# Graph layers with attention: half of the attention stage's lane one-hots kept in DRAM from the adjacency stage

## The chip, the cores and the metric

One core of one Trainium2 chip runs the kernel. The metric is the device time of one execution in microseconds (us). TensorE is PE in the rows (PEld is its weight load), VectorE is DVE, ScalarE is ACT, GpSimd is POOL, and SP is the queue from which most transfers (DMAs) are issued.

## What is computed

There are 3125 nodes of 128 features and 103125 edges, sorted by target. Three rounds of a weighted sparse product are summed and normalised; then a 4-head graph attention over the same edges is added and normalised again.

```python
def spmm(x):                                   # three rounds, summed
    return segment_sum(edge_weight[:, None] * x[src], dst, N)
x = layernorm(x + (x + spmm(x) + spmm(spmm(x)) + ...))
h = (x @ W_node.T).reshape(N, H, HD)           # H = 4, HD = 32
att = leaky_relu(a . [h[src], h[dst], e], 0.2) # per edge and head
m = maximum(segment_max(att, dst), 0)
w = exp(att - m[dst]) / (segment_sum(exp(...)) + (E - deg) * exp(-m))
x = layernorm(x + segment_sum(w * h[src], dst))
```

## The kernel before, in words

Nodes are cut into `NB` = 25 blocks of 128 (a node is block number times 128 plus lane). Nothing is gathered by row: each target has up to 64 edges, and for each block a dense matrix from sources to the block's 128 targets is built on PE out of one-hots. A source id is split into lane (low 7 bits) and block (high bits). DVE compares the lane with 0..127, which gives a lane one-hot of 128 by 32 by 128 elements of two bytes (1 MB) for half a block of targets' edges, and the block with 0..25, which gives a small one-hot; the small one is multiplied by the edges' weights, and PE multiplies lane one-hot by weighted block one-hot. A block has two halves, n = 2j and n = 2j + 1.

The stages follow one another, and each engine has its own hand-written order of instructions, tied by semaphores:

- **Adjacency** (some 90 to 460 us of the span). For each half, DVE's `one_hots` writes `L[n % 4]` (lane, line 1153), `Hh` (1155) and six weighted `Hw[n % 2]` (1163), and raises `lh_ready`. PE's `octet` (607) makes four groups of results for a half, in two PSUM banks; ACT copies each (889) into `rows[j % 2]` and raises `oct_sb`. SP stores the block with four DMAs into `adj` (292); ACT must see that store landed before it writes the same `rows` buffer two blocks later. In between PE, ACT and SP also work on the edge attributes: SP loads them in pairs of DMAs of 992 KB (250), one pair every second block up to block 15. SP also stores each block's source ids (`dup`) into `lh_d` (275).
- **Layers** (to about 880 us): PE multiplies by `adj`, read back in pieces. **Scores** (to about 1075 us): attention terms of the sources.
- **Attention** (to the end). SP loads the ids back (`lhd`, 366). For each half, DVE's `weighted` writes `Lq[n % 2]` (lane again, from the same ids, 1339), `Hq` (1341) and eight `Hx[n % 2]` (1346), and raises `hx_ready`. Around the two halves DVE also does `logits_of`, `finish` and `weights_of` of other blocks. PE's `weights_set` (746) makes 16 sets for a block, 0 to 7 from the even half and 8 to 15 from the odd one, with pieces of the product of the block before (757) between them; after set 8 it turns the next block's weights (732). ACT copies each set (1009), computes exponentials after set 3 and, after set 9, writes the next block's duplicated weights `wdup` (998), on which the next even `weighted` waits.

The odd half's `Lq` holds the same zeros and ones as the odd half's `L` of the adjacency stage; `L` is bf16 and `Lq` fp16. The two waits on which the order around the change rests are in `weighted`:

```python
                if hf == 0:
                    dve.wait_ge(s[f"lhd{j % 3}"], 16 * (j // 3 + 1))
                    dve.wait_ge(s["wdup_sb"], j + 1)
                if n >= 2:
                    dve.wait_ge(s["set_ps"], 8 * (n - 1))
```

Of the kernel before, what the change touches and what calls it, by code (L numbers as in the profile page):

```python
# [36 lines left out]
HP = U // 2  # L37
# [29 lines left out]
def build(nc, x, src, dst, edge_attr, edge_weight, w_node, w_edge, att, out):  # L67
# [5 lines left out]
    rec_d = dram("rec_d", (P * RW + U, REC), BF16)  # L73
    adj = dram("adj", (NB, P, HIP * P), F32)
    lh_d = dram("lh_d", (NB, P, 2 * U * 2), BF16)
    slp = dram("slp", (2, NT, P), BF16)
    z_d = dram("z_d", (E + U, H), F32)
    g_x = [dram(f"g_x{l}", (TBL, D), F32) for l in range(LAYERS + 1)]
# [2 lines left out]
    with ctx:  # L81
# [82 lines left out]
        with ExitStack() as c:  # L164

            Att = [sb(f"Att{i}", [P, H * NB, P], F32, c) for i in range(2)]
            Lq = [sb(f"Lq{i}", [P, HP, P], F16, c) for i in range(2)]
            Hq = sb("Hq", [P, 2, HP, HIP], F16, c)
            Hx = [sb(f"Hx{i}", [P, 2, HP, H, HIP], F16, c) for i in range(2)]
            lhd = sb("lhd", [P, 3, 2, U, 2], BF16, c)  # L170
            zr = sb("zr", [P, 3, U, H], F32, c)
            am = sb("am", [P, 2, H, U], F32, c)
            am2, ex = sb("am2", [P, 2, H, U], F32, c), sb("ex", [P, 2, H, U], F32, c)
            Z16 = sb("Z16", [P, 2, 2, H, P], F16, c)
            wdup = sb("wdup", [P, 2, 2 * H, U, 2], F16, c)
            mx, sm = sb("mx", [P, 2, H], F32, c), sb("sm", [P, 3, H], F32, c)
            fm, fe = sb("fm", [P, 2, 2, H], F32, c), sb("fe", [P, 2, 2, H], F32, c)
            miss = sb("miss", [P, NB], F32, c)
            scale = sb("scale", [P, NB, H], F32, c)
            oT, on = sb("oT", [P, P], F32, c), sb("on", [P, D], F32, c)  # L180
# [3 lines left out]
        names = """lane_set consts clears ld_f ld_d ld_s ld_w ld_wt ld_x ea0 ea1 diag_ready fb_ps fb_sb bad_sb bad_ps flag_ready  # L184
            wp1 wp2 wp3 wr1 wr2 ints rec_out rowi_ready dr0 dr1 dr2 dr3 dr4 dr_used off_ready wt_ps wt_sb
            eaT_ps eaT_sb eaT_used elog_sb
            recs0 recs1 recs2 z_dve z_act clean j_ps dup_sb dup0 dup1 dup2 lh_ready oct_ps oct_sb adj0 adj1
            ld_st ld_sc lohi_sb lohi_ps slt_sb slp_out pc0 pc1 pc2 pc3 pc4 pc5 pc_used yT_sb yt_ps xb_sb y3_sb less_ready squares
            var_ready std_ready x1_ready x1T_ps x1T_sb h_ps h_sb part_ready
            bc0 bc1 bc2 bc3 bh0 bh1 bh2 bh3 lt_ready p4_ps p4_sb  z_ready z_out z_pad pad_out  # L190
# [30 lines left out]
        def _(sp):  # L221
# [55 lines left out]
            def adjacency():  # L277
                store_dup(0)
                store_dup(1)
                for j in range(NB):  # L280
                    if j + 2 < NB:
                        store_dup(j + 2)
                    g = (j + 9) // 2
                    if j % 2 == 1 and EPRE // NC + 2 <= g < NG:
                        sp.wait_ge(s["eaT_ps"], (g - 1) * NC)
                        load_attr(g)
                    sp.wait_ge(s["oct_sb"], 8 * (j + 1))
                    for c in range(2):
# [25 lines left out]
            def layers():  # L314

                sp.wait_ge(s["elog_sb"], NG)
                sp.wait_ge(s["adj0"], 64 * (NB - NB // 2))
                sp.wait_ge(s["adj1"], 64 * (NB // 2))
                for k in range(3):
                    sp.wait_ge(s[f"dup{k}"], 16 * len(range(k, NB, 3)))  # L320
                for n in range(RING):
                    load_piece(n)
                sp.wait_ge(s["ld_sc"], 1)
                edge_tiles(sp, src_t[:, :], src, s["ld_st"])
                for n in range(RING, RING + 5):
                    load_piece(n)
                sp.wait_ge(s["slt_sb"], 14)
                for k in range(2):
                    for q in range(7):
                        r = min(P, NT - q * P)  # L330
                        sp.dma_start(slp[k, q * P:q * P + r, :], slt[0:r, k, q, :]).then_inc(s["slp_out"], 16)
                for n in range(RING + 5, LAYERS * NCH * NPC - 12):
                    load_piece(n)
                sp.wait_ge(s["slp_out"], 16 * 14)
                for h in range(3):
                    load_half(h)
                for n in range(LAYERS * NCH * NPC - 12, LAYERS * NCH * NPC):
                    load_piece(n)
# [19 lines left out]
                    store_half(h)  # L358

            def attention():  # L360
                for j in range(NB):
                    if j >= 3:
                        sp.wait_ge(s["hx_ready"], 2 * (j - 2))
                    else:
                        sp.wait_ge(s["z_out"], 16 * (NH + 1))
                    sp.dma_start(lhd[:, j % 3, :, :, :].rearrange("p q u k -> p (q u k)"), lh_d[j, :, :]).then_inc(s[f"lhd{j % 3}"], 16)
                for k in range(3):
                    b0, b1 = CUT[k], CUT[k + 1]
                    sp.wait_ge(s["y_sb"], b1)
# [175 lines left out]
        def _(pe):  # L545
# [189 lines left out]
            def weights_set(j, q):  # L735
                n, i = 2 * j + q // 8, 16 * j + q
                if q % 8 == 0:
                    pe.wait_ge(s["hx_ready"], n + 1)
                if i >= 3:
                    pe.wait_ge(s["set_sb"], i - 2)  # L740
                for v in range(4):
                    pp = q % 8 * 4 + v
                    for k in range(2):
                        for d in range(2):
                            rows = slice(d * U, (d + 1) * U)
                            m = pe.matmul(bank[i % 3 * 2 + d][:, v * H * NB:(v + 1) * H * NB].rearrange("p (h i) -> p h i", h=H),  # L746
                                          Lq[n % 2][rows, pp, :], Hx[n % 2][rows, k, pp, :, 0:NB], start=(k == 0), stop=(k == 1))
                m.then_inc(s["set_ps"], 1)

            def product(j, lo, hi):  # L750
# [327 lines left out]
        def _(dve):  # L1078
# [67 lines left out]
            def one_hots(n):  # L1146
# [3 lines left out]
                    dve.wait_ge(s["dup_sb"], j + 1)  # L1150
                if n >= LB:
                    dve.wait_ge(s["oct_ps"], 4 * (n - LB + 1))
                dve.tensor_tensor(L[n % LB][:, :, :].rearrange("p u (n k) -> p u n k", k=2), pair_lo, spread(dup[:, j % 3, 0, us, :], P // 2),  # L1153
                                  ALU.is_equal)
                dve.tensor_tensor(Hh[:, n % 2, :, :].rearrange("p u (n k) -> p u n k", k=2), pair_hi,  # L1155
# [153 lines left out]
            def weights_of(j):  # L1309
# [14 lines left out]
                dve.drain()  # L1324
                dve.reciprocal(sm[:, 1, :], sm[:, 0, :])
                dve.drain()
                dve.scalar_tensor_tensor(out=scale[:, j, :], in0=sm[:, 1, :], scalar=1.0 / UP, in1=fe[:, v, 0, :], op0=ALU.mult, op1=ALU.mult)
                dve.drain()
                dve.sem_inc(s["scale_sb"], 1)

            def weighted(n):
# [4 lines left out]
                    dve.wait_ge(s["wdup_sb"], j + 1)  # L1336
                if n >= 2:
                    dve.wait_ge(s["set_ps"], 8 * (n - 1))
                dve.tensor_tensor(Lq[n % 2][:, :, :].rearrange("p u (n k) -> p u n k", k=2), pair_lo, spread(lhd[:, j % 3, 0, us, :], P // 2),  # L1339
                                  ALU.is_equal)  # L1340
                dve.tensor_tensor(Hq[:, n % 2, :, :].rearrange("p u (n k) -> p u n k", k=2), pair_hi,
                                  spread(lhd[:, j % 3, 1, us, :], HIP // 2), ALU.is_equal)
                dve.drain()
# [216 lines left out]
```

## Time and profile before

| what | value |
|---|---|
| runs of the kernel | 1679.84, 1680.29, 1684.0 us; median 1680.29 |
| profiled execution | 1682.1 us, of which the span is 1680.3 us |
| busy over the span | PE 1396.0 us (83%), DVE 1059.3 (63%), ACT 680.2 (40%) |
| mean granted TensorE clock | 0.908 |
| moved by DMA | 250.32 MB |

The span runs from the first to the last instruction of the profiled execution. Busy shares are averages over stages that have different limits, so the stages are read one by one.

### The profile page before, as it was taken

The numbers are of one execution on the slowest core, as the hardware profiler recorded it, in microseconds if no ns is written. First come the engines' busy times: TensorE is split into PE (matmuls) and PEld (weight loads), VectorE is DVE, ScalarE is ACT, GpSimd is POOL, SyncE is SP. The second block draws the span as 40 slices with busy tenths as digits, with TensorE's granted clock in tenths as the row PEclk, the third lists the DMA queues.
The fourth block names the chain that finished last, engine by engine and source line by source line (L and its number), as shares of the span: only waits on it lengthen the run. The fifth ranks groups of instructions, "written<-read, shape, count | busy, mean of one in ns | idle before, by whom it ended". The sixth has DMA issues, their size and how long they took to land.

```text
span 1680.3 us, 50213 instructions
## 1 busy us (share of the span) xinstructions
PE 1396.0 (83%) x22245; PEld 1008.0 (60%) x22245; DVE 1059.3 (63%) x2069; ACT 680.2 (40%) x1575; POOL 140.0 (8%) x102
## 2 busy tenths in 40 slices
PE   4969899986399999999997998567888886888885
PEld 4968789876344454454446888545555554555554
DVE  5499999999500010000116888788888887888873
ACT  3246565654200000001111000166766777677775
POOL 2611101110000000000000000111111011110000
PEclk9999898998799999999997999768888887788887
DMA  5628677755498879969972776200000000000000
GB/s 198 219 94 243 184 212 204 221 145 132 128 348 317 302 282 339 305 213 370 301 257 78 206 217 205 60 11 12 12 11 10 12 12 11 12 9 13 25 3 23
DMA packets 214644, 250.32 MB, mean 149 GB/s; under 512 B 43578, under 2 KB 146487, under 8 KB 214294
## 3 DMA queue, kind: packets, MB, share of 16 engines
q1 hardware_dynamic: 210422, 236.52, 43.6%
q0 software_dynamic: 4000, 10.54, 2.1%
q8 instruction: 177, 2.90, 0.7%
q14 instruction: 45, 0.37, 0.1%
HBM read 197.88 MB, written 49.14 MB: 147 GB/s over the span
## 4 chain that ended last, share of the span: by engine, by line
PE 47%; DVE 31%; DMA 6%; issue 5%; DVEq 4%; ACT 4%; SPq 1%; ACTq 1%; POOL 0%; POOLq 0%
PE bank L680 24%; PE bank L746 9%; PE bank L757 8%; DVE Hw L1163 8%; DVE L L1153 6%; DVE Hx L1346 5%; DVE Lq L1339 4%; DMA lob<-slp 2%; DVE sel L1278 2%; PE bank L717 2%; DMA drow<-in_dst,rowi 2%; DMA hib<-slp 2%; ACT Att L1009 1%; DVEq L1157 1%; DVE Hh L1155 1%
## 5 line engine op out<-in xcount | busy, mean ns | idle before, releaser
L1009 ACT COPY Att<-bank 128x400 f32<-128x400 f32 x800 | 334.9, 540 | 168.2 <-PE bank L746 167.5
L746 PE MATMUL bank<-Hx,Lq 64*128 64x100 f16 x6400 | 241.3, 223 | 88.9 <-DVE Hx L1346 83.3
L746 PEld LDWEIGHTS bank<-Hx,Lq 64*128 64x128 f16 x6400 | 176.6, 102 | 176.3 <-DVE Hx L1346 90.4
L757 PE MATMUL bank<-Att,xa 128*32 128x128 f32 x5000 | 243.0, 307 | 37.8 <-ACT oT L1016 37.8
L607 PE MATMUL bank<-L,Hw 128*52 128x128 bf16 x4800 | 178.1, 233 | 56.2 <-DVE Hw L1163 53.8
L1346 DVE TENSOR_TENSOR Hx<-Hq,wdup 128x832 f16<-128x832 f16 x400 | 205.3, 588 | 4.1 <-issue 0.4
L607 PEld LDWEIGHTS bank<-L,Hw 128*52 128x52 bf16 x4800 | 154.1, 113 | 65.4 <-DVE Hw L1163 58.7
L1163 DVE TENSOR_TENSOR Hw<-Hh,dup 64x832 bf16<-64x832 bf16 x300 | 176.0, 587 | 8.1 <-PE bank L607 1.1
L889 ACT COPY rows<-bank 116x512 f32<-116x512 f32 x200 | 117.2, 586 | 151.2 <-PE bank L607 142.4
L757 PEld LDWEIGHTS bank<-Att,xa 128*32 128x32 f32 x5000 | 123.8, 117 | 77.5 <-ACT Att L1009 41.6
L717 PE MATMUL bank<-Tp,lob 128*128 128x100 bf16 x2418 | 152.5, 210 | 15.6 <-DVE sel L1278 13.6
L717 PEld LDWEIGHTS bank<-Tp,lob 128*128 128x128 bf16 x2418 | 148.1, 99 | 19.1 <-DVE sel L1278 11.7
L484 POOL DMA_INDIRECT zr<-z_d,off x25 | 63.8, 2552 | 1100.0 <-DMA z_d<-elog 704.8
L680 PE MATMUL bank<-pieces,xs 128*128 128x512 f32 (+1 forms) x350 | 138.3, 555 | 17.6 <-DMA pieces<-adj 17.6
L1339 DVE TENSOR_TENSOR Lq<-iota_lo,lhd 128x4096 f16<-128x4096 bf16 x50 | 114.6, 2292 | 55.7 <-PE bank L746 51.4
L719 PE MATMUL bank<-far,hib 128*128 128x100 bf16 x806 | 148.2, 209 | 0.0
L680 PE MATMUL bank<-pieces,xb 128*128 128x512 f32 (+1 forms) x350 | 137.6, 548 | 0.4 <-ACT xb L969 0.4
L680 PE MATMUL bank<-pieces,xa 128*128 128x512 f32 (+1 forms) x350 | 135.6, 547 | 0.4 <-ACT xa L969 0.4
L578 PEld LDWEIGHTS bank<-wedge,eaT 128*128 128x128 f32 (+1 forms) x832 | 127.3, 230 | 1.1 <-issue 0.2
L578 PE MATMUL bank<-wedge,eaT 128*128 128x8 f32 (+1 forms) x832 | 123.6, 273 | 0.0
L924 ACT COPY yT<-bank 128x512 f32<-128x512 f32 (+1 forms) x21 | 11.3, 540 | 269.6 <-PE bank L680 269.6
L680 PEld LDWEIGHTS bank<-pieces,xs 128*128 128x128 f32 x350 | 63.2, 193 | 88.3 <-issue 88.1
(174 smaller groups left out, 1362.8 us busy)
## 6 DMA issues: line engine op xcount, KB each, us to landing
pieces<-adj SPq DMA_DIRECT2D x90, 1280.0 KB, 8.9
adj<-rows SPq DMA_DIRECT2D x100, 416.0 KB
lob<-slp SPq DMA_DIRECT2D x26, 992.0 KB, 6.2
ea<-in_edge_attr SPq DMA_DIRECT2D x25, 992.0 KB, 8.1
hib<-slp SPq DMA_DIRECT2D x78, 64.0 KB, 4.8
pieces<-adj SPq DMA_DIRECT2D x15, 320.0 KB, 3.1
lh_d<-dup SPq DMA_DIRECT2D x25, 64.0 KB, 3.9
lhd<-lh_d SPq DMA_DIRECT2D x25, 64.0 KB, 1.8
```

Source lines behind the costliest of these rows:

```text
L578: m = pe.matmul(bank[7][:, (k * SH + u) * H:(k * SH + u + w) * H], eaT[0:w * DE, q % ER, n * P:(n + 1) * P], wedge[0:w * DE, 0:w * H], sta ...
L607: mm = pe.matmul(bank[m % 2][c * U:c * U + 2 * HIP, v * P:(v + 1) * P], Hw[n % 2][:, k, pp, :, :].rearrange("p d i -> p (d i)"), L[n % LB] ...
L680: m = pe.matmul(bank[n % 2][:, 0:w], cur[:, b, :], rhs, start=(b == 0), stop=(b == NB - 1))
L717: pe.matmul(o, lob[:, h % 4, t * P:(t + 1) * P], Tp[:, k, :, :].rearrange("p h i -> p (h i)"), start=(k == 0), stop=False)
L719: m = pe.matmul(o, hib[:, h % 4, t // 4, :], far[:, t % 4, :, :].rearrange("p h i -> p (h i)"), start=False, stop=True)
L746: m = pe.matmul(bank[i % 3 * 2 + d][:, v * H * NB:(v + 1) * H * NB].rearrange("p (h i) -> p h i", h=H), Lq[n % 2][rows, pp, :], Hx[n % 2][ ...
L757: m = pe.matmul(bank[7][h * HD:(h + 1) * HD, 0:P], xa[:, i, h * HD:(h + 1) * HD], Att[j % 2][:, h * NB + i, :], start=(i == 0), stop=(i == ...
L889: act.copy(rows[j % 2][0:U + 2 * HIP, hf * 4 + o, :, :].rearrange("p v n -> p (v n)"), bank[m % 2][0:U + 2 * HIP, :])\
L1009: m = act.copy(o[:, d, :, :], bank[i % 3 * 2 + d][:, 0:4 * H * NB].rearrange("p (q i) -> p i q", q=4))
L1163: m = dve.tensor_tensor(Hw[n % 2][rows, k, :, d, :].rearrange("p u (n k) -> p u n k", k=2), Hh[rows, n % 2, :, :].rearrange("p u (n k) -> ...
L1339: dve.tensor_tensor(Lq[n % 2][:, :, :].rearrange("p u (n k) -> p u n k", k=2), pair_lo, spread(lhd[:, j % 3, 0, us, :], P // 2), ALU.is_equal)
L1346: m = dve.tensor_tensor(Hx[n % 2][:, k, :, h, :].rearrange("p u (n k) -> p u n k", k=2), Hq[:, n % 2, :, :].rearrange("p u (n k) -> p u n ...
```

## The change

In the adjacency stage each odd half's lane one-hot, `L[1]` or `L[3]`, is stored to a new DRAM tensor `lo_d` by SP, before the block's `adj` stores. DVE may write that `L` buffer again, two blocks later, only when its store has landed. In the attention stage DVE writes only the even `Lq`; the odd one is loaded by SP from `lo_d`, once PE has used the odd half before it, and PE's set 8 waits for it. The bits of bf16 1.0 read as fp16 are 1.875, so `Lq` is now bf16, PE reads it as fp16, and the final scale is divided by 1.875. SP issues the loads of ids two blocks ahead of the `Lq` loads. Nothing else of the computation changes.

```diff
+    lo_d = dram("lo_d", (NB, P, HP * P), BF16)
...
-            Lq = [sb(f"Lq{i}", [P, HP, P], F16, c) for i in range(2)]
+            Lq = [sb(f"Lq{i}", [P, HP, P], BF16, c) for i in range(2)]
...
                         load_attr(g)
+                    sp.wait_ge(s["lh_ready"], 2 * j + 2)
+                    sp.dma_start(lo_d[j, :, :], L[(2 * j + 1) % LB][:, :, :].rearrange("p u n -> p (u n)"))\
+                        .then_inc(s[f"lo_out{(2 * j + 1) % LB}"], 16)
                     sp.wait_ge(s["oct_sb"], 8 * (j + 1))
...
             def attention():
-                for j in range(NB):
+                def ids_in(j):
...
+                ids_in(0)
+                ids_in(1)
+                for j in range(NB):
+                    if j + 2 < NB:
+                        ids_in(j + 2)
+                    if j:
+                        sp.wait_ge(s["set_ps"], SETS * j)
+                    sp.dma_start(Lq[1][:, :, :].rearrange("p u n -> p (u n)"), lo_d[j, :, :]).then_inc(s["lo_in"], 16)
...
                     pe.wait_ge(s["hx_ready"], n + 1)
+                    if n % 2:
+                        pe.wait_ge(s["lo_in"], 16 * (j + 1))
...
                     dve.wait_ge(s["oct_ps"], 4 * (n - LB + 1))
+                    if n % 2:
+                        dve.wait_ge(s[f"lo_out{n % LB}"], 16 * (n // LB))
...
-                dve.tensor_tensor(Lq[n % 2][:, :, :].rearrange("p u (n k) -> p u n k", k=2), pair_lo, spread(lhd[:, j % 3, 0, us, :], P // 2),
-                                  ALU.is_equal)
+                if hf == 0:
+                    dve.tensor_tensor(Lq[0][:, :, :].rearrange("p u (n k) -> p u n k", k=2), pair_lo, spread(lhd[:, j % 3, 0, us, :], P // 2),
+                                      ALU.is_equal)
```

SP's queue in the adjacency stage, from the ids' store of one block to that of the next, where a pair of attribute loads (`ea`) falls. Before:

```order
L275 DMA lh_d<-dup 128x256 [waits dup_sb]
L250 DMA ea<-in_edge_attr_64 128x1984 [waits eaT_ps]
L250 DMA ea<-in_edge_attr_64 128x1984
L292 DMA adj<-rows1 26x32x128 [waits oct_sb]
L292 DMA adj<-rows1 26x32x128 x3
```

and now:

```order
L277 DMA lh_d<-dup 128x256 [waits dup_sb]
L252 DMA ea<-in_edge_attr_64 128x1984 [waits eaT_ps]
L252 DMA ea<-in_edge_attr_64 128x1984
L290 DMA lo_d<-L3 128x4096 [waits lh_ready]
L297 DMA adj<-rows1 26x32x128 [waits oct_sb]
L297 DMA adj<-rows1 26x32x128 x3
```

The 1 MB store stands in front of the block's four `adj` stores, with a wait of its own.

DVE in the attention stage, from one even half's `weighted` through `logits_of` to the odd half's, now:

```order
L1360 TENSOR_TENSOR Lq0<-iota_lo,lhd 128x4096 [waits set_ps,wdup_sb,lhd1]
L1362 TENSOR_TENSOR Hq<-iota_hi,lhd 128x832
L1367 TENSOR_TENSOR Hx0<-Hq,wdup 128x32x26 x8
L1310 TENSOR_TENSOR am<-zr,sdst 128x256 [waits e_sb,zr0]
...
L1325 TENSOR_SCALAR fm<-mx 128x4
L1362 TENSOR_TENSOR Hq<-iota_hi,lhd 128x832 [waits set_ps]
L1367 TENSOR_TENSOR Hx1<-Hq,wdup 128x32x26 x8
```

Before, a row `Lq1<-iota_lo,lhd` stood ahead of the second `Hq`, and the wait on `set_ps` was on it.

SP's queue at the start of the attention stage, now:

```order
L373 DMA lhd<-lh_d 128x256 [waits z_out] x3
L382 DMA Lq1<-lo_d 128x4096
L373 DMA lhd<-lh_d 128x256 [waits hx_ready]
L382 DMA Lq1<-lo_d 128x4096 [waits set_ps]
L373 DMA lhd<-lh_d 128x256 [waits hx_ready]
L382 DMA Lq1<-lo_d 128x4096 [waits set_ps]
```

Before, only the loads of `lhd` stood there, with the same waits.

## Rows read from the trace of the kernel before

**Rows 1.** Busy time of each engine by stretch: two adjacency blocks, then attention.
```profile
core 0: us, PE busy (x) PEld busy (x) DVE busy (x) ACT busy (x) POOL busy (x), PEclk, DMA share, GB/s
126.00:154.00 28.00, 26.40 (x538) 24.74 (x538) 27.21 (x39) 17.97 (x37) 3.48 (x2) 1.00 0.82 230
...
1060.00:1660.00 600.00, 459.71 (x11674) 319.23 (x11671) 489.89 (x1010) 402.38 (x977) 63.80 (x25) 0.83 0.05 13
```

**Rows 2.** Waits from 1060 to 1660 us: total us, times, longest.
```profile
PE bank L746 <- DVE Hx L1346: 83.3, 27, 11.0
...
DVE Lq L1339 <- PE bank L746: 51.4, 23, 7.4
```

**Rows 3.** Timelines of DVE, PE and ACT in an attention block: start, us, idle before.
```profile
1310.87 2.29 DVE L1339 TENSOR_TENSOR Lq<-iota_lo,lhd 128x4096 f16<-128x4096 bf16 x1 [2.31 <-PE bank L746]
...
1317.90 0.85 PE L746 MATMUL bank<-Hx,Lq 64*128 64x100 f16 x16 [2.76 <-DVE Hx L1346]
...
1320.87 2.29 DVE L1339 TENSOR_TENSOR Lq<-iota_lo,lhd 128x4096 f16<-128x4096 bf16 x1
...
1323.74 4.11 DVE L1346 TENSOR_TENSOR Hx<-Hq,wdup 128x832 f16<-128x832 f16 x8
...
1329.00 0.54 PE L746 MATMUL bank<-Hx,Lq 64*128 64x100 f16 x16
...
1331.74 1.04 ACT L998 CAST wdup<-bank 128x1024 f16<-128x1024 f32 x1
```

**Rows 4.** Timeline at set 8 of attention's first block, and of block 14.
```profile
1108.36 0.85 PE L746 MATMUL bank<-Hx,Lq 64*128 64x100 f16 x16 [2.79 <-DVE Hx L1346]
...
1111.35 1.03 ACT L998 CAST wdup<-bank 128x1024 f16<-128x1024 f32 x1
...
1428.61 0.54 PE L746 MATMUL bank<-Hx,Lq 64*128 64x100 f16 x16 [2.40 <-DVE Hx L1346]
...
1433.05 2.29 DVE L1339 TENSOR_TENSOR Lq<-iota_lo,lhd 128x4096 f16<-128x4096 bf16 x1 [1.35 <-ACT wdup L998]
```

**Rows 5.** Groups by line, 1060 to 1660 us: the lane one-hots.
```profile
L1339 DVE TENSOR_TENSOR Lq<-iota_lo,lhd 128x4096 f16<-128x4096 bf16 x50 | 114.6, 2292 | 55.7 <-PE bank L746 51.4 <-ACT wdup L998 1.4 <-issue 0.2
```

**Rows 6.** Timeline of SP's queue in two adjacency blocks: start, us spent issuing.
```profile
238.98 1.34 SPq L250 DMA_DIRECT2D ea<-in_edge_attr  x2
240.58 13.42 SPq L292 DMA_DIRECT2D adj<-rows  x4
...
258.31 5.54 SPq L292 DMA_DIRECT2D adj<-rows  x4
```

**Rows 7.** Stretches of the adjacency stage, columns as in rows 1.
```profile
240.60:247.60 7.00, 6.22 (x125) 5.75 (x125) 6.81 (x10) 4.21 (x9) 2.31 (x1) 1.00 0.93 301
...
277.50:294.00 16.50, 15.00 (x247) 13.99 (x246) 16.11 (x21) 8.18 (x17) 2.45 (x1) 0.79 0.71 191
...
347.00:361.00 14.00, 11.94 (x247) 11.07 (x243) 13.61 (x20) 8.49 (x18) 2.73 (x1) 1.00 0.51 134
```

**Rows 8.** DMA busy tenths in 40 slices of 268:296 (with GB/s), then of 449:460.
```profile
DMA  4959999998888994776676688677868744765120
GB/s 126 187 197 374 397 363 363 329 329 305 265 271 252 275 307 140 206 189 154 185 200 179 143 244 223 154 166 206 191 181 253 244 138 140 195 174 148 40 88 6
...
DMA  0566666666667767777887665326777666651000
```

**Rows 9.** Chain that ended last, from 85 to 480 us: start, us, what.
```profile
347.97 2.29 DVE L L1153
...
362.12 2.29 DVE L L1153
...
452.73 6.87 DMA adj<-rows
```

**Rows 10.** Waits from 95 to 460 us: total us, times, longest.
```profile
ACT rows L889 <- DMA adj<-rows: 4.5, 4, 1.5
...
DVE Hw L1163 <- PE bank L607: 1.1, 2, 0.7
```

**Rows 11.** DMA issues: count, KB each, median us to landing.
```profile
ea<-in_edge_attr SPq DMA_DIRECT2D x25, 992.0 KB, 8.1
```

More of the change, by code:

```diff
@@ L57 @@
 UP = float(2 ** 14)
+ONE = 1.875
 FAR = -float(2 ** 127)
@@ L186, in build @@
             eaT_ps eaT_sb eaT_used elog_sb
-            recs0 recs1 recs2 z_dve z_act clean j_ps dup_sb dup0 dup1 dup2 lh_ready oct_ps oct_sb adj0 adj1
+            recs0 recs1 recs2 z_dve z_act clean j_ps dup_sb dup0 dup1 dup2 lh_ready lo_out1 lo_out3 lo_in oct_ps oct_sb adj0 adj1
             ld_st ld_sc lohi_sb lohi_ps slt_sb slp_out pc0 pc1 pc2 pc3 pc4 pc5 pc_used yT_sb yt_ps xb_sb y3_sb less_ready squares
@@ L320, in layers @@
                     sp.wait_ge(s[f"dup{k}"], 16 * len(range(k, NB, 3)))
+                sp.wait_ge(s["lo_out1"], 16 * (NB - NB // 2))
+                sp.wait_ge(s["lo_out3"], 16 * (NB // 2))
                 for n in range(RING):
@@ L746, in weights_set @@
                             m = pe.matmul(bank[i % 3 * 2 + d][:, v * H * NB:(v + 1) * H * NB].rearrange("p (h i) -> p h i", h=H),
-                                          Lq[n % 2][rows, pp, :], Hx[n % 2][rows, k, pp, :, 0:NB], start=(k == 0), stop=(k == 1))
+                                          Lq[n % 2][rows, pp, :].bitcast(F16), Hx[n % 2][rows, k, pp, :, 0:NB], start=(k == 0), stop=(k == 1))
                 m.then_inc(s["set_ps"], 1)
@@ L1326, in weights_of @@
                 dve.drain()
-                dve.scalar_tensor_tensor(out=scale[:, j, :], in0=sm[:, 1, :], scalar=1.0 / UP, in1=fe[:, v, 0, :], op0=ALU.mult, op1=ALU.mult)
+                dve.scalar_tensor_tensor(out=scale[:, j, :], in0=sm[:, 1, :], scalar=1.0 / (ONE * UP), in1=fe[:, v, 0, :], op0=ALU.mult, op1=ALU.mult)
                 dve.drain()
```

## The prediction, made before the changed kernel ran

> **What bounds the kernel now.** I read the busy time by stage first. In the adjacency stage DVE is busy 27.21 of 28 us, and the DMA engines 0.82 of the time; in attention DVE is the busiest too, but with 489.89 of 600 us it has gaps [rows 1]. So the two stages that the change touches have different limits, and I follow each by its waits.
>
> In attention the waits say who holds whom: PE waits for DVE's `Hx` 83.3 us, in only 27 waits for 50 halves, and DVE's `Lq` waits 51.4 us, in 23 [rows 2]. One block shows why [rows 3]. The even `Lq` starts at 1310.87; `Hq` and `Hx` follow, and PE's set 0 starts at 1317.90, after 2.76 us without work. The odd `Lq` starts at 1320.87, and the odd `Hx` are done at 1323.74 + 4.11 = 1327.85. PE comes to set 8 only at 1329.00, without having waited. After sets 8 and 9 ACT writes `wdup`, done at 1331.74 + 1.04 = 1332.78, and only then can the next even `Lq` start. (The row at 1310.87 names PE as releaser of its 2.31 us wait, but PE's even sets were long done; in the program that instruction waits for `wdup` as well.) The loop of a block is therefore even `Lq`, `Hx`, sets 0 to 9, `wdup`. The odd `Lq` hangs beside it, with 1.15 us to spare.
>
> In adjacency I read DVE's step from the chain: `L` of two blocks starts at 347.97 and 362.12, so a block takes 14.15 us [rows 9].
>
> **The change, part by part.**
>
> *25 odd `Lq` go from DVE.* One takes 2.292 us [rows 5], so DVE loses 57.3 us of work. In a block like that of rows 3 all of it lies beside the loop: the odd `Hx` are ready 2.3 us sooner, PE arrives at set 8 when it did, and DVE waits for `wdup` longer. I cost these blocks at nothing; what is next late there is still the even half. The odd half is on the path where PE stood at set 8: in the first block, 2.79 us, and in block 14, 2.40 us, behind the first normalisation [rows 4]. There the whole 2.29 us comes out, because `wdup` follows set 9 directly (1111.35 after a set 8 at 1108.36; `Lq` at 1433.05 after a set 8 at 1428.61). **Minus 4.6 us.** The bounds are 0 and minus 5.2 (the two waits whole).
>
> *25 loads of 1 MB into `Lq[1]`.* SP issues one when PE has done the odd half before, some 14 us ahead of the set 8 that needs it (set 15 ends just before the 2.76 us without work that end at 1317.90, and set 8 is at 1329.00 [rows 3]). A load of 992 KB lands in 8.1 us in the median, amid other traffic [rows 11]; attention moves 13 GB/s [rows 1]. I take nothing. The bounds are 0 and, if it took over 14 us, the excess in each block. The loads of ids keep their waits, and what waits behind them in SP's queue is only the output's stores, due at the end. The even `Lq` is of the same width as before: nothing. The scale's constant: nothing.
>
> *25 stores of 1 MB in adjacency.* This is the dear part. DVE issues nothing for them, and its new wait (for a store two blocks old) has 28 us. But they stand in SP's queue before the `adj` stores, and that queue is nearly full. The last block's `adj` stores, with nothing beside them, keep the DMA engines at 6 to 7 tenths for 36 slices of 0.275 us, which is 9.9 us [rows 8]; so 6 to 7 tenths is what these stores look like at full speed. Behind a pair of attribute loads two blocks' stores run back to back at the same 0.71 [rows 7]. Over 268 to 296 us, which is one pair of attribute loads and two blocks' stores, data flows without a break but for about the last 2.5 us [rows 8]: 25.5 us of work in 28.3 us. SP is held back accordingly: it needs 13.42 us to issue one block's four stores behind the attributes [rows 6].
>
> A store of 1.05 MB takes 3.5 us at the 301 GB/s of the attribute loads [rows 7] and 2.6 us at the highest slice, 397 GB/s [rows 8]. I take 2.7, near the slice, since in a full queue the start of one transfer hides behind the one before. Two blocks then ask for 25.5 + 2 x 2.7 = 30.9 us of 28.3: 2.6 us too much, in each of the eight pairs of blocks that load attributes: 21 us. After block 16 a block asks for 9.9 + 2.7 and a little for ids, under 14.15, so there it costs nothing.
>
> Not all of the 21 us reaches DVE. Late `adj` stores hold ACT at the `rows` buffer, ACT holds PE, and PE holds DVE, which may be a half-block ahead: 7 us. ACT itself has some 2 us, since it waited only 4.5 us so far, and DVE's `Hw` waited for PE 1.1 us in the whole stage [rows 10]. So **plus 21 - 9 = 12 us.** The bounds: 0, if the stores slip into the third of the engines' time that rows 8 show free; and 34 us, with 3.5 us a store (8 x 4.2) and no cushion.
>
> The Trainium skill (DMA: Bandwidth & Descriptors, Specifications) gives a ceiling of 435 GB/s, and by it a store would take 2.4 us, an estimate from that page. The excess would be 2.0 us a pair, the cost 16 - 9 = 7 us and the whole change +2.4 us. The trace's 301 GB/s stay well below that ceiling.
>
> The end of the stage: the last `adj` stores land 6.87 us after their last issue [rows 9]; the last 1 MB store is issued before them, while PE works on the last half, and I give it nothing.
>
> *Sum:* 12 - 4.6 = +7.4 us. The profiled execution took 1682.1 us, with a span of 1680.3, so it would take 1689.5; it stood 1.8 us above the median of the runs. From the median, 1680.29 + 7.4 = **1687.7 us**.
>
> **The rivals.**
>
> *The stores cost nothing.* If the idle third of the engines' time during `adj` stores can be used, only the 4.6 us are left: 1675.7 us, so not slower. For it: the mean DMA share of a block without attributes is only 0.51 [rows 7]. Against it: the 0.71 behind the attributes, where the queue was full. It decides as soon as a store takes under some 2 us of the queue's time (21 becomes 9, the cushion).
>
> *No cushion.* PE waits more, and has no time to catch up: its granted clock is 0.79 in one such stretch already, so part of it at the lower of its two levels, 1.2 and 2.4 GHz [rows 7]. That is +34 - 4.6 = 1709.7 us at the most; I put it at 1704.
>
> *The load is late.* If `lo_in` came 2 us after PE reaches set 8, 24 blocks would lose 2 us each: 1724 us. A load would have to take over 14 us where 8.1 is the median in worse traffic.
>
> *DVE's work counts in full.* 57.3 us less, 1623 us. It needs every odd `Hx` to hold PE; the counts of rows 2 (27 waits, 25 blocks) and the 1.15 us to spare in rows 3 contradict it. The Trainium skill (Trace Analysis, Identifying the Most-Contended Engine) would lead here: it says to take the engine with the highest occupancy as the most contended and to optimise it first, and that is DVE in attention. On the waits, this trace does not agree.
>
> **How the numbers follow.** A measurement of this kernel tells 0.3%, 5 us, from no change. The forecast case has a chance of 0.47 and runs from 1682 to 1698; of it 0.38 lies above 1685.3 and 0.09 in the middle. Free stores have 0.36: 0.22 within 5 us of before, 0.14 below it. No cushion has 0.12, a late load 0.03, DVE in full 0.02. That makes faster 0.16, same 0.31, slower 0.53. The range goes from 1675 (free stores) to 1704 (no cushion); it leaves out the last two rivals, the best of the free stores and the upper end of the third.
>
> **What would show it.** In the changed kernel: attention blocks of the same length, DVE's wait before the even `Lq` some 2.3 us longer, and no wait at set 8 in the first block and in block 14. In adjacency: more than 4.5 us of ACT waiting for `adj<-rows`, DVE's `Hw` or `L` waiting for PE, and the stage's end some 12 us later, all of it before block 17. I am wrong if the pieces of `adj` start by 460 us as before (free stores), or if PE waits for a DMA at set 8.

## The result, and the profile after

| what | before | after |
|---|---|---|
| median of 10 runs each | 1679.68 us | 1689.74 us |
| lowest to highest | 1677.49 to 1684.0 | 1686.15 to 1693.98 |
| profiled execution | 1682.1 us (span 1680.3) | 1693.98 us (span 1692.2) |
| busy: PE, DVE, ACT | 1396.0, 1059.3, 680.2 us | 1392.8, 1005.0, 675.8 us |
| moved by DMA | 250.32 MB | 302.77 MB |

The ratio is 1.0059, with a 95% interval of 1.0046 to 1.0072: slower by 9.9 us (7.7 to 12.1). The profiled executions stand above their medians, by 2.4 us before and by 4.2 us after, so the traces show some 2 us more as lost than the medians do.

DVE has 54 us less to do and the kernel is slower. The two stages tell why, one at a time.

**Adjacency.** First the end of the stage, the issue of the first pieces of `adj`, in SP's timelines (start, us spent issuing). Before:

```profile
459.65 11.31 SPq L300 DMA_DIRECT2D pieces<-adj  x6
```

After (with the first and the last block that load attributes, and some of the blocks behind them):

```profile
130.25 12.86 SPq L297 DMA_DIRECT2D adj<-rows  x4
...
345.38 12.47 SPq L297 DMA_DIRECT2D adj<-rows  x4
...
362.34 10.03 SPq L297 DMA_DIRECT2D adj<-rows  x4
...
376.01 6.69 SPq L297 DMA_DIRECT2D adj<-rows  x4
...
388.15 9.40 SPq L297 DMA_DIRECT2D adj<-rows  x4
...
477.69 10.37 SPq L305 DMA_DIRECT2D pieces<-adj  x6
```

The stage ends 18.0 us later. The rows of blocks 1 and 15 lie seven pairs of blocks apart: (345.38 - 130.25) / 7 = 30.73 us a pair. The same two in the kernel before, with blocks 3 and 16:

```profile
129.52 10.30 SPq L292 DMA_DIRECT2D adj<-rows  x4
...
155.25 9.56 SPq L292 DMA_DIRECT2D adj<-rows  x4
...
325.04 8.68 SPq L292 DMA_DIRECT2D adj<-rows  x4
...
339.20 7.82 SPq L292 DMA_DIRECT2D adj<-rows  x4
```

That is 27.93 us a pair: 2.8 us less on the mean. The first of these pairs took only 25.73 us (129.52 to 155.25); the six behind it took (325.04 - 155.25) / 6 = 28.30 us each, which is DVE's pace of 2 x 14.15. In block 16, SP is 362.34 - 339.20 = 23.1 us behind. From block 17 on it catches up, with a step of 12 us from block 17 to 18 (376.01 to 388.15) where DVE's block takes 14.15.

Who waits for the late queue is in the waits of after, from 95 to 475 us (total us, times, longest):

```profile
ACT rows L907 <- DMA adj<-rows: 66.5, 16, 8.3
...
DVE L L1173 <- DMA lo_d<-L: 13.4, 6, 3.2
...
DVE Hw L1183 <- PE bank L623: 4.8, 7, 1.1
...
DVE L L1173 <- PE bank L623: 1.0, 1, 1.0
```

ACT waits 66.5 us for `adj` stores, where it had waited 4.5 [rows 10]. DVE, which had waited 1.1 us in the whole stage, now waits 13.4 + 4.8 + 1.0 = 19.2 us: 18.1 more, which is the 18.0 of the stage's end. Most of it is its own new wait, for the store of `lo_d`. Where it lies is in DVE's timeline; these are `L` of the even halves of blocks 18 and 19:

```profile
364.06 2.29 DVE L1173 TENSOR_TENSOR L<-iota_lo,dup 128x4096 bf16<-128x4096 bf16 x1
...
380.18 2.29 DVE L1173 TENSOR_TENSOR L<-iota_lo,dup 128x4096 bf16<-128x4096 bf16 x1
```

Blocks 18 and 19 stood at 347.97 and 362.12 [rows 9]: 16.1 and 18.1 us late. The whole 18 us are reached only here, three blocks behind the last attribute load. A row of the DMA issues of 268 to 296 us, the stretch of [rows 8] (count, KB each, median us to landing):

```profile
lo_d<-L SPq DMA_DIRECT2D x2, 1024.0 KB, 9.5
```

A store of one-hots takes 9.5 us from issue to landing there.

**Attention.** The waits from 1080 to 1680 us of after:

```profile
DVE Lq L1360 <- PE bank L764: 84.1, 23, 8.6
PE bank L764 <- DVE Hx L1367: 79.1, 26, 10.6
...
DVE Z L1335 <- ACT Z L1009: 15.3, 20, 0.9
```

DVE waits 32.7 us longer ahead of the even `Lq` (51.4 in [rows 2]), and PE only 4.2 us less for `Hx`. DVE's wait for ACT's `Z` (15.3 us in 20 waits) is new: it comes to it sooner than ACT has it ready. Together these two take up 48.0 of the 57.3 us that DVE no longer works. A steady block of after, in the timelines of DVE and PE, to hold against [rows 3]:

```profile
1303.66 2.29 DVE L1360 TENSOR_TENSOR Lq<-iota_lo,lhd 128x4096 bf16<-128x4096 bf16 x1 [3.73 <-PE bank L764]
...
1310.69 0.85 PE L764 MATMUL bank<-Hx,Lq 64*128 64x100 f16 x16 [2.76 <-DVE Hx L1367]
...
1314.33 4.11 DVE L1367 TENSOR_TENSOR Hx<-Hq,wdup 128x832 f16<-128x832 f16 x8
...
1325.65 2.29 DVE L1360 TENSOR_TENSOR Lq<-iota_lo,lhd 128x4096 bf16<-128x4096 bf16 x1 [3.44 <-PE bank L764]
```

From even `Lq` to odd `Hx` it now takes 1314.33 - 1303.66 = 10.67 us (12.87 in rows 3), but from one even `Lq` to the next 21.99; PE still stands 2.76 us at set 0. The blocks that did change are seen in PE's set 0. Before, blocks 0, 1, 2, 14 and 15:

```profile
1098.37 1.85 PE L746 MATMUL bank<-Hx,Lq 64*128 64x100 f16 x40 [10.99 <-DVE Hx L1346]
...
1119.50 0.85 PE L746 MATMUL bank<-Hx,Lq 64*128 64x100 f16 x16 [4.15 <-DVE Hx L1346]
...
1140.81 0.85 PE L746 MATMUL bank<-Hx,Lq 64*128 64x100 f16 x16 [3.12 <-DVE Hx L1346]
...
1406.71 0.85 PE L746 MATMUL bank<-Hx,Lq 64*128 64x100 f16 x16 [2.76 <-DVE Hx L1346]
...
1440.08 0.85 PE L746 MATMUL bank<-Hx,Lq 64*128 64x100 f16 x16 [2.00 <-DVE Hx L1346]
```

The same blocks after, and set 8 of block 0 behind the first row:

```profile
1117.02 1.18 PE L764 MATMUL bank<-Hx,Lq 64*128 64x100 f16 x24 [10.62 <-DVE Hx L1367]
...
1124.83 0.54 PE L764 MATMUL bank<-Hx,Lq 64*128 64x100 f16 x16 [0.68 <-DVE Hx L1367]
...
1135.64 0.85 PE L764 MATMUL bank<-Hx,Lq 64*128 64x100 f16 x16 [4.15 <-DVE Hx L1367]
...
1155.55 0.54 PE L764 MATMUL bank<-Hx,Lq 64*128 64x100 f16 x16 [2.77 <-DVE Hx L1367]
...
1421.46 0.54 PE L764 MATMUL bank<-Hx,Lq 64*128 64x100 f16 x16 [2.77 <-DVE Hx L1367]
...
1452.47 0.54 PE L764 MATMUL bank<-Hx,Lq 64*128 64x100 f16 x16 [2.77 <-DVE Hx L1367]
```

Block 0 is shorter by 2.5 us (21.13 to 18.62), block 1 by 1.4 (21.31 to 19.91), block 14 by 2.4 (33.37 to 31.01); that is 6.3 of the 6.7 us by which set 0 of block 24 comes sooner after the first (541.76 us before, 535.05 after). So the profiled execution reads: plus 18.0 in adjacency, minus 6.7 in attention, and 0.6 more in between and at the end, 11.9 in the span.

### The profile page after: what moved, and what is told of

It reads as the page before. It is cut to its first block, busy times and chain, and to the rows that moved or that the text cites. A ratio compares the mean times of both kernels' runs of the same rounds, so it can differ in the third digit from the quotient of the medians.

```text
span 1692.2 us, 50262 instructions
## 1 busy us (share of the span) xinstructions
PE 1392.8 (82%) x22245; PEld 1006.4 (59%) x22245; DVE 1005.0 (59%) x2044; ACT 675.8 (40%) x1575; POOL 97.2 (6%) x102
## 2 busy tenths in 40 slices
DMA packets 221846, 302.77 MB, mean 179 GB/s; under 512 B 44378, under 2 KB 147287, under 8 KB 215094
## 4 chain that ended last, share of the span: by engine, by line
PE 49%; DVE 17%; SPq 13%; DMA 8%; ACT 5%; issue 4%; DVEq 3%; ACTq 1%; POOL 0%; POOLq 0%
PE bank L696 23%; SPq L297 9%; PE bank L764 9%; PE bank L775 8%; DVE Hx L1367 5%; DVE Lq L1360 3%; PE bank L733 3%; DMA hib<-slp 2%; DMA adj<-rows 2%; DVE Hw L1183 2%; PE bank L623 2%; ACT Att L1027 2%; DMA drow<-in_dst,rowi 2%; DVE L L1173 2%; DVE sel L1298 1%
## 5 line engine op out<-in xcount | busy, mean ns | idle before, releaser
L623 PE MATMUL bank<-L,Hw 128*52 128x128 bf16 x4800 | 183.4, 237 | 71.2 <-ACT rows L907 35.5
L623 PEld LDWEIGHTS bank<-L,Hw 128*52 128x52 bf16 x4800 | 159.8, 116 | 80.3 <-ACT rows L907 37.1
L733 PEld LDWEIGHTS bank<-Tp,lob 128*128 128x128 bf16 x2418 | 147.0, 99 | 19.3 <-DVE sel L1298 10.9
L594 PEld LDWEIGHTS bank<-wedge,eaT 128*128 128x128 f32 (+1 forms) x832 | 123.8, 224 | 1.0
L1173 DVE TENSOR_TENSOR L<-iota_lo,dup 128x4096 bf16<-128x4096 bf16 x50 | 114.6, 2292 | 15.7 <-DMA lo_d<-L 13.4
L1360 DVE TENSOR_TENSOR Lq<-iota_lo,lhd 128x4096 bf16<-128x4096 bf16 x25 | 57.3, 2293 | 85.8 <-PE bank L764 84.1
```

The lines of the kernel that those rows point to most:

```text
L594: m = pe.matmul(bank[7][:, (k * SH + u) * H:(k * SH + u + w) * H], eaT[0:w * DE, q % ER, n * P:(n + 1) * P], wedge[0:w * DE, 0:w * H], sta ...
L623: mm = pe.matmul(bank[m % 2][c * U:c * U + 2 * HIP, v * P:(v + 1) * P], Hw[n % 2][:, k, pp, :, :].rearrange("p d i -> p (d i)"), L[n % LB] ...
L733: pe.matmul(o, lob[:, h % 4, t * P:(t + 1) * P], Tp[:, k, :, :].rearrange("p h i -> p (h i)"), start=(k == 0), stop=False)
```

## The experiments

Each was timed beside the kernel before on the same chip; a difference in us is the ratio less one, times the median of before there (1679 to 1681).

**1. The stores alone**

```diff
-                    sp.dma_start(Lq[1][:, :, :].rearrange("p u n -> p (u n)"), lo_d[j, :, :]).then_inc(s["lo_in"], 16)
-                        pe.wait_ge(s["lo_in"], 16 * (j + 1))
-                if hf == 0:
-                    dve.tensor_tensor(Lq[0][:, :, :].rearrange("p u (n k) -> p u n k", k=2), pair_lo, spread(lhd[:, j % 3, 0, us, :], P // 2),
+                dve.tensor_tensor(Lq[n % 2][:, :, :].rearrange("p u (n k) -> p u n k", k=2), pair_lo, spread(lhd[:, j % 3, 0, us, :], P // 2),
```

> The stores of the changed kernel alone: attention is as before, with all 50 `Lq` written by DVE and no loads. If the change is two separate parts (my theory), the stores cost by themselves what the trace of after shows in adjacency: the pieces of `adj` start 12 to 18 us later than 459.65 us, attention has its old length (541.8 us from the first to the last even `Lq`), and the time is 1692 to 1698 us. If the stores only hurt together with the loads or the new waits of attention, or if the profiled execution of after was merely a long one, the pieces start within 5 us of 460 and the time is 1680 to 1685.

Measured: 1697.59 us, ratio 1.0095 (1.0075 to 1.0115): plus 16.0 us. The pieces start at 478.81, attention from set 0 of block 0 to that of block 24 takes 541.3 us. The stores by themselves cost more than the whole change loses.

**2. The loads alone**

```diff
-                    sp.wait_ge(s["lh_ready"], 2 * j + 2)
-                    sp.dma_start(lo_d[j, :, :], L[(2 * j + 1) % LB][:, :, :].rearrange("p u n -> p (u n)"))\
-                        .then_inc(s[f"lo_out{(2 * j + 1) % LB}"], 16)
+                    if j == 0:
+                        sp.wait_ge(s["lh_ready"], 2)
+                        sp.dma_start(lo_d[0, :, :], L[1][:, :, :].rearrange("p u n -> p (u n)")).then_inc(s["lo_out1"], 16)
...
+                    sp.dma_start(Lq[1][:, :, :].rearrange("p u n -> p (u n)"), lo_d[0, :, :]).then_inc(s["lo_in"], 16)
```

> The loads alone: only block 0's one-hots are stored, and every block loads those (the odd halves of the other blocks are computed with block 0's lane one-hots, so that part of the computation is left out). By my theory attention alone is left of the change: the pieces of `adj` start within 1 us of 459.65, attention is shorter by 4.6 us (my forecast) to 6.7 us (the trace of after), and the time is 1673 to 1675.5 us. The rival, that DVE's removed work counts in full (57 us), gives 1623; the rival that the loads themselves hold attention up gives 1680 or more, with PE waiting for a DMA before set 8.

Measured: 1675.3 us, ratio 0.9965 (0.9952 to 0.9978): minus 5.9 us. The pieces start at 459.31. The two halves of the change add up: 16.0 - 5.9 = 10.1, where the whole gave 9.9. No load is waited for, and a cut of 57 us in DVE's work is worth 6.

**3. Only the two blocks that gain**

```diff
+KEPT = (0, 14)
...
+                    if j in KEPT:
+                        sp.wait_ge(s["lh_ready"], 2 * j + 2)
...
+                if hf == 0 or j not in KEPT:
```

(The loads, PE's wait and DVE's wait have the same condition.)

> Store and load in blocks 0 and 14 only; the other 23 blocks write both `Lq` by DVE as before. By my theory only the blocks where PE stood at set 8 gain from the load: 2 x 2.3 = 4.6 us, at most 5.7 with the quicker block 1 after it, and two stores cost at most 1 us of adjacency, so 1674.5 to 1676.5 us, and this version is faster than both kernels. If instead all 25 blocks give a little (the 6.7 us of after in 25 pieces of 0.27), two blocks give 0.5 us and the time is that of before, 1679 to 1680.

Measured: 1674.98 us, ratio 0.9967 (0.9954 to 0.9979): minus 5.5 us. Two loads of 25 give what 25 give, and this version beats both kernels. Block 0 shows it in PE's timeline, sets 0 and 8, then set 0 of block 1:

```profile
1102.34 4.75 PE L768 MATMUL bank<-Hx,Lq 64*128 64x100 f16 x112 [10.98 <-DVE Hx L1371]
1110.13 0.85 PE L768 MATMUL bank<-Hx,Lq 64*128 64x100 f16 x16 [0.66 <-DVE Hx L1371]
...
1121.27 0.85 PE L768 MATMUL bank<-Hx,Lq 64*128 64x100 f16 x16 [3.84 <-DVE Hx L1371]
```

PE's wait at set 8 is 0.66 us where it was 2.79 [rows 4], and the block takes 18.93 us for 21.13.

**4. The change with room in the queue**

```diff
+                    c = SH * DE if g < EPRE // NC + 2 else DE
-                    sp.dma_start(ea[:, buf, k, :, :].rearrange("p u d -> p (u d)"), view[k]).then_inc(s[f"ea{buf}"], 16)
+                    sp.dma_start(ea[:, buf, k, :, :].rearrange("p u d -> p (u d)")[:, 0:c], view[k][:, 0:c]).then_inc(s[f"ea{buf}"], 16)
```

> The whole change, but the attribute loads of the adjacency stage bring one row of attributes per partition instead of 32 (most of the edge attributes of the later groups are left out). It takes some 2 MB out of every pair of blocks and leaves every wait and the order of SP's queue as they are. If the stores cost because the queue is full of bytes (my theory), the cost goes: DVE's `L` of the even halves is 14.2 us apart throughout, ACT waits for `adj<-rows` no more than 5 us, the pieces start at 458 to 462 us and the time is 1672 to 1676. If they cost by their place ahead of the `adj` stores, by the wait for both halves' one-hots or by DVE's wait for a store two blocks old, the pieces still start at 470 us or later and the time is 1685 to 1692.

Measured: 1676.4 us, ratio 0.9967 (0.9954 to 0.998): minus 5.5 us, the loads' gain alone. ACT's wait and a stop of PE, from the waits of 95 to 475 us:

```profile
ACT rows L908 <- DMA adj<-rows: 4.1, 3, 1.7
...
PE bank L624 <- issue: 4.3, 2, 3.3
```

All 25 stores are still made, from the same place and with the same waits, and ACT waits 4.1 us in place of 66.5. The pieces start at 462.85, 0.85 us outside what I expected; the 3.2 us over before come in one place, with a stop of PE of 3.33 us for nothing that the profile shows. So it is the bytes beside the attribute loads that cost.

**5. The store behind the `adj` stores**

```diff
-                    sp.wait_ge(s["lh_ready"], 2 * j + 2)
-                    sp.dma_start(lo_d[j, :, :], L[(2 * j + 1) % LB][:, :, :].rearrange("p u n -> p (u n)"))\
-                        .then_inc(s[f"lo_out{(2 * j + 1) % LB}"], 16)
                     sp.wait_ge(s["oct_sb"], 8 * (j + 1))
...
+                    sp.wait_ge(s["lh_ready"], 2 * j + 2)
+                    sp.dma_start(lo_d[j, :, :], L[(2 * j + 1) % LB][:, :, :].rearrange("p u n -> p (u n)"))\
+                        .then_inc(s[f"lo_out{(2 * j + 1) % LB}"], 16)
```

> The whole change with one move: SP issues a block's one-hot store behind the block's four `adj` stores and not ahead of them. If the bytes cost (my theory: two blocks ask the queue for 30.7 us where DVE gives it 28.3), the order is of no account: the pieces of `adj` start at 471 to 481 us and the time is 1685 to 1693 us. If the store cost because it stood in the way of the `adj` stores, these are issued as before, ACT waits for `adj<-rows` under 10 us, the pieces start at 460 to 466 and the time is 1672 to 1680.

Measured: 1728.77 us, ratio 1.0277 (1.0246 to 1.0308), and the pieces start at 515.20. Both theories missed. SP's timeline in block 1, and DVE's odd `L` of block 3, which needs that block's buffer:

```profile
130.10 11.92 SPq L294 DMA_DIRECT2D adj<-rows  x4
142.06 0.59 SPq L297 DMA_DIRECT2D lo_d<-L  x1
```

```profile
149.90 2.29 DVE L1173 TENSOR_TENSOR L<-iota_lo,dup 128x4096 bf16<-128x4096 bf16 x1 [3.61 <-DMA lo_d<-L]
```

The store is issued at 142.06 (129.78 in the whole change), DVE starts 7.8 us after that, when it has landed, and had stood 3.61 us by then: 49.7 us in 13 waits over the stage. ACT's wait for `adj<-rows` is not among this stage's waits any more, so I read the queue as having room and DVE as held by the way from one-hots to PE to ACT to the `adj` stores' issue to the store's landing; no run takes that way apart. The place ahead of the `adj` stores is the better one, and I had seen neither why nor by how much.

**6. Six `L` buffers**

```diff
-LB = 4
+LB = 6
...
+                dve.wait_ge(s["lo_out5"], 16 * 8)
                 dve.memset(src_t[:, (NH - 1) * SH:NT], 0)
```

> The whole change with six `L` buffers for four, so that DVE waits for a store three blocks old and not two. In the trace of after SP's issues fall 23 us behind before, DVE 18 us; I had taken 9 us of cushion and there were 5. Theory A: DVE's own wait for the store (13.4 us) goes past ACT and PE and takes the cushion away; without it the loss is 23 - 9 = 14 us, the pieces start at 473 to 475 and the time is 4 us under that of after, 1684 to 1687. Theory B: the wait is only the place where the full queue shows first; its time goes to DVE's `Hw` waiting for PE (4.8 us in after, then 12 or more), the pieces start at 476 to 479 and the time is 1688 to 1692.

Measured: 1691.83 us, ratio 1.0065 (1.0046 to 1.0084); the pieces start at 478.51. Its waits, 95 to 475 us:

```profile
ACT rows L907 <- DMA adj<-rows: 63.5, 15, 9.2
...
DVE Hw L1183 <- PE bank L623: 19.3, 11, 4.3
```

DVE's wait for the store is gone, and its wait for PE is 19.3 us: the same sum as the 19.2 of after. Theory B holds: the queue takes its time from DVE by whichever way is shorter.

**7. Stores where no attributes are loaded**

```diff
+KEPT = tuple(range(17, 25))
```

> Store and load in blocks 17 to 24 only, where SP loads no attributes. My theory: there the queue has room (in after SP's step from one block's `adj` stores to the next is 12.1 to 12.8 us in blocks 18 to 21, where DVE's is 14.15), so eight stores cost 0 to 1 us, and the loads of steady attention blocks give nothing: 1678 to 1683 us, the pieces at 459 to 462. The rival, that every store costs its transfer of 2.7 us even in a queue with room, gives 8 x 2.7 = 22 us more, 1702. If the last store delays the last `adj` stores, the pieces are 2 to 3 us later and only they.

Measured: 1681.05 us, ratio 1.0003 (0.9991 to 1.0015); the pieces start at 460.06. Eight stores cost nothing that can be measured, and eight loads in steady blocks give nothing (set 0 of block 0 to that of block 24 takes 542.1 us, 541.76 before).

**8. The kernel before, with the even half early**

```diff
                 if hf == 0:
                     dve.wait_ge(s[f"lhd{j % 3}"], 16 * (j // 3 + 1))
-                    dve.wait_ge(s["wdup_sb"], j + 1)
...
+                if hf == 0:
+                    dve.wait_ge(s["wdup_sb"], j + 1)
                 dve.drain()
```

> The kernel before, without any store or load of one-hots; in `weighted` the wait for `wdup` stands behind the even `Lq` and `Hq` and not ahead of them, so that DVE makes these two (2.29 + 0.58 us) while it would wait. My reading of the loop (even `Lq`, `Hx`, sets 0 to 9, `wdup`) says that this, and not the odd `Lq`, shortens every block: by what DVE waited there, 51.4 us in 23 waits, so some 45 to 51 us come out and the time is 1629 to 1636 us; DVE's wait before the even `Lq` is nearly gone, and PE's wait for `Hx` falls from 83 to 25 to 40 us. If the loop were held by something else (PE's sets, ACT's copies, the ids), the time stays at 1675 to 1681.

Measured: 1632.5 us, ratio 0.9708 (0.9679 to 0.9736): minus 49 us, with no transfer at all. Its stretch from 1120 to 1360 us, columns as in rows 1, and its waits in attention:

```profile
1120.00:1360.00 240.00, 204.55 (x5541) 140.56 (x5539) 223.01 (x459) 187.73 (x453) 35.20 (x12) 0.92 0.05 13
```

```profile
PE bank L746 <- DVE Hx L1347: 58.1, 36, 10.9
...
DVE Lq L1338 <- PE bank L746: 2.3, 6, 1.3
```

This is the loop of [rows 3] put to use: the even `Lq` and `Hq` were on it. DVE's 51.4 us of waiting are 2.3 now, and DVE is busy 93% of the stretch. PE still waits 58.1 us, more than the 25 to 40 I expected: it is now held at both halves (36 waits).

**9. The whole change, with the even half early** (the edit of experiment 8 on the changed kernel)

```diff
-                    dve.wait_ge(s["wdup_sb"], j + 1)
...
+                if hf == 0:
+                    dve.wait_ge(s["wdup_sb"], j + 1)
                 dve.drain()
```

> The whole change, and the wait for `wdup` behind the even `Lq` and `Hq` as in the kernel with the even half early. There DVE no longer waits in attention (a block takes 20.3 us, all of it DVE's work), so now the odd `Lq`, 2.29 us, should lie on the path in every block. My theory: DVE-bound blocks of 18.0 to 18.5 us; attention 46 to 55 us shorter than in that kernel, stores +16 us in adjacency, so 1632.5 - 50 + 16 = 1594 to 1604 us. The rival: without the odd `Lq` PE's sets or the loop over `wdup` bound at once, blocks of 19.5 to 20 us, and only blocks 0 and 14 gain in full: 1630 to 1643 us.

Measured: 1604.88 us, ratio 0.9548 (0.9525 to 0.957), 0.9 us above what I expected. The same stretch and its waits:

```profile
1120.00:1360.00 240.00, 212.55 (x5896) 148.47 (x5892) 218.59 (x494) 203.75 (x496) 17.23 (x14) 0.94 0.22 72
```

```profile
PE bank L764 <- DVE Hx L1368: 25.1, 17, 10.6
```

A block takes 18.35 us (mean of blocks 2 to 13) against 20.4 in experiment 8. The first set to the last is 468.6 us for 512.7, so the removed `Lq` give 44 us, and the pieces start 15 us later, at 474.88. The same change that costs 10 us in the kernel of this study is worth some 27 us (a ratio of 0.9548 for 0.9708) where DVE is the bound.

**10. One store in each pair of blocks**

```diff
+KEPT = tuple(range(0, 17, 2))
```

> Store and load in the even blocks 0 to 16 only (nine stores, one in each pair of blocks that loads attributes), attention's order as before. By my sum a pair has 28.3 - 25.5 = 2.8 us of the queue free, and one store asks for some 2.7 (2.8 per two in excess gives the same): half the stores in these blocks cost 0 to 3 us, not half of 16, and the blocks 0 and 14 give their 5 to 6: 1674 to 1678 us, the pieces at 459 to 463. If the cost is in proportion to the number of stores, 9 x 0.65 = 6 us, less 5.8: 1680 to 1682, the pieces at 465 to 468.

Measured: 1676.23 us, ratio 0.9977 (0.9965 to 0.9988): minus 3.9 us; the pieces start at 457.89, and ACT waits 5.0 us for `adj<-rows`. Against the minus 5.5 of the two blocks alone, nine stores cost about 1.6 us, inside the intervals of both, and not in proportion. The 2.8 us that a pair has free by the forecast's sum (28.3 - 25.5) take in one store.

**11. One store in a pair, all late ones, and the even half early** (KEPT of experiments 10 and 7 together, with the edit of 8)

```diff
+KEPT = tuple(range(0, 17, 2)) + tuple(range(17, 25))
...
-                    dve.wait_ge(s["wdup_sb"], j + 1)
...
+                if hf == 0:
+                    dve.wait_ge(s["wdup_sb"], j + 1)
                 dve.drain()
```

> Store and load in the even blocks 0 to 16 and in all of 17 to 24 (17 of 25), with the even `Lq` and `Hq` ahead of the wait for `wdup`. My theory: the stores cost 0 to 3 us (the queue has room for one in a pair with attributes, and for all after them), and each of the 17 blocks gives 1.8 to 2.3 us where DVE is the bound: 1632.5 - 35 + 2 = 1592 to 1603 us, as fast as the whole change with the early even half or faster. If PE or the loop over `wdup` binds at once, the time is 1624 to 1630.

Measured: 1605.45 us, ratio 0.955 (0.9526 to 0.9573), 2.5 us above what I expected. The stores are as cheap as meant (pieces at 460.76), but attention gives only 25.7 us (487.0 for 512.7) for 17 loads, 1.5 a block. In its waits PE stands 38.8 us for `Hx` in 22 waits. From set 0 to set 0, in blocks 2 to 13, a block with a load takes 18.6 to 19.8 us and one without 20.3; in blocks 17 to 22, all with a load, it is 18.3 to 18.8 us. So the blocks between that still write both `Lq` hold the time up. It is no faster than the whole change with the same edit.

## Why the prediction was right, and where its terms were off

The forecast, 1687.7 us, is 2 us from the measured 1689.74, by the way that it named: the stores fill SP's queue beside the attribute loads, and attention gains mainly in the blocks where PE stood at set 8. That it came so near is partly luck. Adjacency cost 16.0 us (experiment 1) for the forecast 12, and attention gave 5.9 (experiment 2) for 4.6; the two errors, 4.0 and 1.3 us, partly cancel, and the kernel before was 0.6 us faster in these runs than the 1680.29 from which the forecast started.

*The queue.* I reckoned 30.9 us for a pair of blocks; it is 30.73. A store therefore takes (30.73 - 25.5) / 2 = 2.6 us of a full queue, and I had 2.7. Against the 28.30 us of steady pairs before, that is 2.4 us too much in a pair (forecast: 2.6); with the short first pair the backlog came to 23.1 us, and I had 21. The Trainium skill (DMA: Bandwidth & Descriptors, Specifications) gives the ceiling of 435 GB/s by which I estimated 2.4; the 2.6 are 1.05 MB at 400 GB/s, so here its ceiling is nearer than the 301 GB/s that the attribute loads showed. Experiments 1 and 4 put the cost on the bytes, 7 and 10 show that a queue with room takes a store for nothing (0.5 us in all, inside the interval) or little (1.6 us for nine).

*The cushion* is the term that failed: "21 - 9 = 12". SP came 23.1 us behind and DVE 18.1, so the cushion was 5 us and not 9; the stores cost 16.0 us by experiment 1, and 18.0 in the profiled execution of after, which is one of the longer ones. I had added 7 us of DVE's lead, half a block, and 2 of ACT's. The 13.4 us of DVE's new wait suggest that it goes past both; experiment 6 took that wait away and the loss stayed, so it is not the reason. The traces show what is. In the kernel before, PE's work on the even half of block 18, between attribute work, and the start of DVE's `Hw` for the even half of block 19, which overwrites what PE reads there:

```profile
354.48 0.86 PE L607 MATMUL bank<-L,Hw 128*52 128x128 bf16 x24 [1.79 <-DVE Hw L1163]
...
358.91 1.53 PE L607 MATMUL bank<-L,Hw 128*52 128x128 bf16 x48
```

```profile
364.99 3.58 DVE L1163 TENSOR_TENSOR Hw<-Hh,dup 64x832 bf16<-64x832 bf16 x6
```

PE is done at 358.91 + 1.53 = 360.44, so it may be 364.99 - 360.44 = 4.55 us late before DVE stands. My 7 us had left out that PE itself needs 6 us for a half. ACT's first copy of block 17, which waits for the `adj` stores of block 15, before and after:

```profile
341.29 0.59 ACT L889 COPY rows<-bank 116x512 f32<-116x512 f32 x1 [1.36 <-PE bank L607]
```

```profile
364.47 0.58 ACT L907 COPY rows<-bank 116x512 f32<-116x512 f32 x1 [8.31 <-DMA adj<-rows]
```

SP began to issue those stores 20.3 us late (345.38 for 325.04), and the copy is 23.2 us late, so nothing of ACT's 2 us is seen there. The 5 us from there to DVE's 18.1 come close to DVE's lead of 4.55.

*DVE's wait for the store* was given 28 us. That is the time between two writes of a buffer, not the slack. In experiment 5 DVE wanted the buffer of block 1 at 149.90 - 3.61 = 146.3; from the issue at 129.78 in the whole change that is 16.5 us, of which a landing takes 9.5 where the queue is full. The wait cost nothing of its own there (experiment 6); with the issue 12.3 us later, the pieces start 37.5 us later than in the whole change (experiment 5).

*"After block 16 it costs nothing"* is true of the stores there (experiment 7), but the backlog of 23 us is worked off in these blocks, and DVE's loss still grew from 16.1 us in block 18 to 18.1 in block 19.

*Attention* was put at minus 4.6 us and gives 5.9 by experiment 2, 6.7 in the trace. Blocks 0 and 14 gave 2.5 and 2.4 for the forecast 2.29 each. The 1.4 us of block 1 I had not seen, and their cause was not tried; that block also took only 20.9 us (21.31 before) in the traces of experiments 1 and 3, where it loads nothing, so some of it is not the load's. Steady blocks came as said (22.16 us on the mean of blocks 2 to 13 in both traces), and so did the loads. Two signs did not: the wait ahead of the even `Lq` grew by 1.4 us each (32.7 us in 23 waits) and not by 2.3, the wait for `Z` taking its share, and set 8 of block 0 still waits, 0.68 us.

*The rivals.* Free stores are excluded by experiment 1. With no cushion all 23.1 us of the backlog would have reached DVE and not 18.1 (the 34 us of that rival also took 3.5 us a store): the result lies between that rival and the forecast. No load was late. DVE's work in full fell here, and experiments 8 and 9 show its condition: with the even half early DVE's wait ahead of `Lq` is down to 2.3 us, and then the same 57 us count with 44. So the rule of the Trainium skill that I set against the waits (Perfetto Trace Analysis, Identifying the Most-Contended Engine) fails here at a DVE busy 82% of attention [rows 1], and holds at 93% (experiment 8).

## What to carry to other kernels

Before moving work from an engine, ask whether that engine ever waits in the stage: here 57 us of its work were worth 6 us while it waited 51 us behind one semaphore, and 44 us once two instructions had been moved ahead of that wait. Price a transfer by how full the queue is where it is issued: 2.6 us each in the stretches that have no room, nothing that could be measured in blocks without other loads; so place it in the blocks that have room, and keep it only where someone waits for what it replaces. A buffer's slack is the time from the issue of what reads it to the moment at which its writer wants it again, less the landing, and not the time from write to write. And an engine's lead over the next one is what its step leaves after the next one's own work: 4.6 us here, where I had taken half a step, 7.

## What the runs showed of the hardware that I had not expected

TensorE's granted clock was higher where PE was kept waiting less. From 1120 to 1360 us it was 0.92 of full speed in experiment 8 and 0.94 in experiment 9, and 0.85 in the kernel before, so more of that stretch was at 2.4 GHz and less at 1.2:

```profile
1120.00:1360.00 240.00, 198.17 (x5108) 135.09 (x5102) 204.59 (x421) 171.95 (x417) 32.25 (x11) 0.85 0.04 12
```

PE was busy 198.17 us of it before, 204.55 in experiment 8 and 212.55 in experiment 9. Part of what those two versions gain may come from the clock; no run here separates it.

The DMA engines' busy share is a poor sign of how full a queue is. Over the seven pairs of blocks with attributes, in the kernel before, in experiment 10 (one store a pair) and in the whole change, columns as in rows 1:

```profile
129.50:325.00 195.50, 179.09 (x3418) 166.83 (x3412) 190.03 (x265) 117.63 (x231) 26.28 (x14) 0.94 0.72 208
```

```profile
129.50:325.00 195.50, 173.74 (x3403) 161.72 (x3401) 189.67 (x264) 117.42 (x231) 31.63 (x14) 0.97 0.81 248
```

```profile
130.00:345.00 215.00, 181.85 (x3454) 169.47 (x3454) 195.73 (x272) 115.70 (x233) 22.89 (x15) 0.90 0.84 258
```

The share is 0.81 where the queue still keeps DVE's pace and 0.84 where it falls behind in every pair; the sixth that seems free at 0.84 was not used. What told was SP's step from pair to pair.
